# A DLRM tower on one core: gathered rows in buffers of their own, w1 loaded elsewhere, middle shelves by broadcast, and new orders on all engines

## What is computed

```python
e = jnp.stack([tbl_0[ids[:, 0]], ..., tbl_38[ids[:, 38]]], axis=1)   # (2048, 39, 64)
s = jnp.sum(e, axis=-1)                                            # (2048, 39)
z = s[:, _ROW] * s[:, _COL]                                        # all 741 pairs
h = jnp.concatenate([z, dense_ctx], axis=1)                        # (2048, 757)
h = jnp.maximum(h @ W_top1 + b_top1, 0.0)                          # 512
h = jnp.maximum(h @ W_top2 + b_top2, 0.0)                          # 256
y = h @ W_top3
```

## Time and profile before

| | |
|---|---|
| three executions | 318.14, 319.54, 319.74 us |
| profiled execution, span | 314.8 us (its own total isn't given beside it; the median is 4.7 us above the span) |
| TensorE busy | 207.8 us (66%), 1659 matmuls |
| VectorE busy | 144.2 us (46%) |
| ScalarE busy | 81.2 us (26%) |
| GpSimd busy | 114.8 us (36%), of which gathers 112.2 |
| DMA | 43.70 MB, mean 139 GB/s |
| TensorE clock granted, mean | 0.782 of full |

### The profile page before, as it was taken

How to read it: one execution, slowest core, us unless ns; L and a number is a source line. 1 busy time by engine, 2 the same in 40 slices (tenths; PEclk the granted TensorE clock), 3 DMA queues, 4 the chain that set the end, 5 groups by cost and what they waited for, 6 DMA issues and landing times.

```text
span 314.8 us, 4373 instructions
## 1 busy us (share of the span) xinstructions
PE 207.8 (66%) x1659; PEld 126.9 (40%) x1659; DVE 144.2 (46%) x384; ACT 81.2 (26%) x144; POOL 114.8 (36%) x124
## 2 busy tenths in 40 slices
PE   0652102499794321118956988856999999999996
PEld 0310000344131100004613655653566776667784
DVE  2000000157990000002964679561589988968440
ACT  0200010268980000000064224210132424035432
POOL 6777777000077777740473320537310000000000
PEclk9955555589667555555985999977599999999999
DMA  7811131189924132115693676999124029100000
GB/s 290 286 29 30 27 93 25 46 300 413 418 87 129 25 69 89 25 21 186 221 342 121 217 254 218 350 351 244 25 60 150 2 77 275 52 2 2 2 0 0
DMA packets 13557, 43.70 MB, mean 139 GB/s; under 512 B 3216, under 2 KB 4256, under 8 KB 13408
## 3 DMA queue, kind: packets, MB, share of 16 engines
q1 hardware_dynamic: 9392, 39.42, 36.1%
q0 software_dynamic: 3712, 3.81, 5.8%
q10 hardware_dynamic: 432, 0.19, 0.2%
HBM read 43.14 MB, written 0.27 MB: 138 GB/s over the span
## 4 chain that ended last, share of the span: by engine, by line
PE 51%; issue 31%; DVE 7%; ACT 5%; another core or an unknown queue 3%; DMA 2%; ACTq 0%; DVEq 0%
PE g L1119 8%; PE ph L1226 8%; PE ph L1227 7%; PE ph L1230 6%; PE ph L1119 5%; PE s L1205 3%; DVE mid_sums L505 2%; PE g L1165 2%; PE g L1102 2%; PE ph L1246 2%; PE g L1140 2%; DMA stage<-early 2%; PE ph L1250 2%; PE ph L1247 2%
## 5 line engine op out<-in xcount | busy, mean ns | idle before, releaser
L429 POOL DMA_INDIRECT rows<-tab,idc x68 | 65.8, 968 | 77.9 <-DVE w_lo L522 32.8
L438 POOL DMA_INDIRECT rows<-tab,idc x48 | 46.4, 968 | 36.7 <-DVE bsum L587 18.4
L1119 PE MATMUL g<-stage,fc 128*32 128x100 f32 x378 | 27.3, 318 | 41.2 <-issue 40.2
L1119 PE MATMUL ph<-stage,fc 128*32 128x96 f32 (+2 forms) x378 | 20.9, 285 | 39.9 <-issue 30.6
L1226 PE MATMUL ph<-z_hi,w_hi 126*128 126x512 f32 (+1 forms) x96 | 44.8, 467 | 0.0
L536 DVE TENSOR_SCALAR hots<-hots,fc 125x2048 bf16<-125x2048 bf16 x28 | 20.7, 751 | 43.6 <-issue 42.5
L1227 PE MATMUL ph<-z_hi,w_lo 126*128 126x512 f32 (+1 forms) x96 | 39.7, 413 | 0.7 <-issue 0.7
L1230 PE MATMUL ph<-z_lo,w_hi 126*128 126x512 f32 (+1 forms) x96 | 39.3, 409 | 0.0
L1119 PEld LDWEIGHTS g<-stage,fc 128*32 128x32 f32 x378 | 15.8, 139 | 52.6 <-issue 50.9
L1119 PEld LDWEIGHTS ph<-stage,fc 128*32 128x32 f32 x378 | 12.4, 134 | 49.1 <-issue 47.9
L478 DVE CAST mparts<-g 125x100 bf16<-125x100 f32 x3 | 0.8, 262 | 62.4 <-PE g L1119 50.4
(11 more groups left out here) (88 smaller groups left out, 269.0 us busy)
## 6 DMA issues: line engine op xcount, KB each, us to landing
stage<-middle SPq DMA_DIRECT2D x17, 800.0 KB
hots<-shelf_scratch SPq DMA_DIRECT2D x17, 512.0 KB
stage<-early SPq DMA_DIRECT2D x3, 768.0 KB
stage<-middle SPq DMA_DIRECT2D x3, 750.0 KB
stage<-early SPq DMA_DIRECT2D x3, 640.0 KB
rows<-tab,idc POOLq DMA_INDIRECT x116
slot_b<-slot_scratch SPq DMA_DIRECT2D x8, 224.0 KB
stage<-early SPq DMA_DIRECT2D x3, 512.0 KB
```

The costliest lines, as they stand in the source:

```text
L429: pool.indirect_dma_start(rows[:, n % ROW_RING, i, :], None, gathered[i], bass.IndirectOffsetOnAxis(ap=idc[:, n, i:i + 1], axis=0)).then_i ...
L438: pool.indirect_dma_start(rows[:, n % ROW_RING, i, :], None, gathered[i], bass.IndirectOffsetOnAxis(ap=idc[:, n, i:i + 1], axis=0)).then_i ...
L1119: mm = pe.matmul(bank[j * LANE:(j + 1) * LANE, 0:w], band, stage[:, q, (r * 4 + j) * w:(r * 4 + j + 1) * w], start=(x == 0), stop=(x == PA ...
```

## The change

- The gathered rows get buffers of their own: `rows_two` (two buffers of four tiles for the middle tables, chunk by chunk in turn) and `rows_l` (sixteen tiles for the large ones, no reuse). `asum` and `bsum` are doubled. Each tile has its own semaphore.
- Chunk 1's middle gathers wait for all six parts of w1 (before: five). Chunk 2's and 3's middle gathers wait once, for all four sums of the chunk two before; large gathers wait for no sum.
- Raw w1 goes to `factors`, `mid_picked`, `rows_l` and `rows_two[1]` in four transfers, early in SyncE's list; w2 too.
- Middle shelves come by broadcast DMA from a scratch of their own (`mid_scratch`) for all chunks; the five spreads of middle fields on TensorE and their copies on ScalarE go.
- Chunk 2's slots are spread by TensorE and copied by ScalarE, like those of chunks 0 and 1; only chunk 3's come by DMA.
- The lists of all engines are written in another order. Outputs y lie in `rows_l`.

```diff
-        rows = sb("rows", [P, ROW_RING, NL, DIM], F32)
-        asum = sb("asum", [P, TILES, NA], F32)
+        rows_two = [sb(f"rows_m{c}", [P, TILES, NA - SUMMED[c], DIM], F32) if SUMMED[c] < NA else None for c in (0, 1)]
+        rows_m = [rows_two[c % 2][:, :, 0:NA - SUMMED[c], :] if SUMMED[c] < NA else None for c in range(CHUNKS)]
+        rows_l = sb("rows_l", [P, ROW_RING, NB, DIM], F32)
+        asum = sb("asum", [P, 2, TILES, NA], F32)
...
             def load_weights():
-                sp.dma_start(w1_early, w1[:, 0:(KCH - 1) * H1]).then_inc(w1_in, 16)
-                sp.dma_start(w1_raw[KCH - 1], w1[:, (KCH - 1) * H1:]).then_inc(w1_last_in, 16)
+                for k in (0, 1):
+                    sp.dma_start(w1_raw[k], w1[:, k * H1:(k + 1) * H1]).then_inc(w1_in[k], 16)
+                sp.dma_start(w1_mid, w1[:, 2 * H1:5 * H1]).then_inc(w1_in[2], 16)
+                sp.dma_start(w1_raw[5], w1[:, 5 * H1:]).then_inc(w1_in[3], 16)
...
             def load_mid_shelves(c):
-                if SUMMED[c - 1]:
-                    sp.wait_ge(mid_looked_up, (4, 8, 12, 16)[c - 1])
-                sp.wait_ge(shelf_out, 16)
+                if mid_looks(c):
+                    sp.wait_ge(mid_looked_up, mid_looks(c))
+                sp.wait_ge(mid_out, 16)
+                sp.dma_start(mid_hots[:, 0:SUMMED[c], :],
+                             mid_dram[c * NA:c * NA + SUMMED[c], :].rearrange("(o f) n -> o (f n)", o=1)
+                             .partition_broadcast(P)).then_inc(mid_hots_in, 16)
...
-            def fetch_a(c, t):
-                n = c * TILES + t
-                if c == 1 and t == 0:
-                    pool.wait_ge(w1_split, KCH - 1)
-                if c >= 2:
-                    pool.wait_ge(a_summed, n - ROW_RING + 1)
+            def fetch_a(c, a, b):
+                if c == 1:
+                    pool.wait_ge(w1_split, KCH)
+                elif c >= 2:
+                    pool.wait_ge(a_summed, (c - 1) * TILES)
+                for x in range(a, b):
+                    t, i = divmod(x, NA - SUMMED[c])
...
+            def fetch_b(c, a, b):
                 if c >= 2:
-                    pool.wait_ge(b_summed, n - ROW_RING + 1)
+                    pool.wait_ge(w1_split, 5)
...
-SLOT_SPREAD = 2
+SLOT_SPREAD = 3
...
+            load_table(0, 2)
+            load_dense()
+            load_select()
+            load_table(0, 1)
+            load_table(0, 0)
             load_ids()
-            load_table(0, 0)
-            load_table(0, 1)
-            load_table(0, 2)
+            load_mid_ids()
+            load_weights2()
             load_table(0, 3)
+            load_weights()
```

More of the change, by code:

```diff
@@ L257, in hot_loads, with mid_looks @@
             return sum(not spread_group(v // GROUPS, v % GROUPS) for v in range(u % HOTS, u + 1, HOTS))
[L259 to L269, removed]
+        def mid_looks(c):
+            return sum(len(LOOK_PARTS[x]) for x in range(c) if SUMMED[x]) * TILES
         def selects(c, which):
@@ L587, in sum_b @@
-                dve.tensor_reduce(bsum[:, t, 0:NB], rows[:, slot, NA:, :], AX.X, ALU.add).then_inc(b_summed, 1)
+                n = c * TILES + t
+                dve.wait_ge(rows_b_in[n], 16 * NB)
+                dve.tensor_reduce(bsum[:, c % 2, t, 0:NB], rows_l[:, n % ROW_RING, :, :], AX.X, ALU.add).then_inc(b_summed, 1)
             def split_a(c):
                 dve.wait_ge(cleared, 1)
-                dve.wait_ge(a_summed, (c + 1) * TILES)
+                if SUMMED[c] < NA:
+                    dve.wait_ge(a_summed, sum(SUMMED[x] < NA for x in range(c + 1)) * TILES)
@@ L643, in _ @@
+            split_w1(1)
+            hot(0, 2)
+            split_w1(2)
+            split_w1(3)
+            mid_hot(0)
+            split_tables(1)
+            slot_copy(0, 4, G0)
+            sum_a(0, 1)
+            split_w1(4)
+            split_w1(5)
+            pick(0, 1, G1)
+            slot_copy(0, 5, G0)
             hot(0, 3)
-            pick(0, 2, G0)
+            pick(0, 2, G1)
             hot(0, 4)
+            slot_copy(0, 6, G0)
+            hot(0, 5)
+            split_tables(2)
@@ L812, in _ @@
-            mid_pick(3, 0, 0, 5, G1, 13)
-            z_low(2, 3)
-            multiply(2, 5)
-            z_low(2, 4)
-            sum_a(3, 1)
-            z_low(2, 5)
-            dve.wait_ge(mid_picked_ready, 40)
-            mid_pick(3, 1, 0, 5, G0, 14)
+            hot(3, 6)
+            sum_a(3, 1)
+            pick(3, 1, G0)
+            pick(3, 2, G1)
+            z_low(2, 3)
+            z_low(2, 4)
+            multiply(2, 5)
+            sum_a(3, 2)
+            sum_a(3, 3)
+            pick(3, 3, G0)
@@ L820, in _ @@
+            pick(3, 4, G1)
+            z_low(2, 5)
+            pick(3, 5, G0)
+            pick(3, 6, G1)
+            mid_hot(3)
+            sum_b(3, 0)
+            dve.wait_ge(mid_picked_ready, 35)
+            mid_pick(3, 0, 0, 5, G0, 13)
+            multiply(3, 0)
+            multiply(3, 1)
+            dve.wait_ge(mid_picked_ready, 40)
+            mid_pick(3, 1, 0, 5, G1, 14)
+            z_low(3, 0)
+            h1_low(2, 0)
+            h1_low(2, 1)
+            h1_low(2, 2)
             dve.wait_ge(mid_picked_ready, 45)
@@ L1835 @@
     by_field = np.zeros((P, CHUNK), ids.dtype)
+    mid_by_field = np.zeros((CHUNKS * NA, CHUNK), ids.dtype)
     for c in range(CHUNKS):
@@ L1838 @@
         by_field[c * LANE:c * LANE + NE] = part[:, EARLY].T
-        for i in range(SUMMED[c]):
-            by_field[mid_row(c, i)] = part[:, MIDDLE[i]]
+        mid_by_field[c * NA:(c + 1) * NA] = part[:, MIDDLE].T
     by_row = ids[:, MIDDLE + LARGE].reshape(BATCH // P, P, NL).transpose(1, 0, 2)
```

1025 lines of the change are left out of this document (521 added, 504 removed).

## The result

Five executions of the changed kernel took 334.14 us (median; 333.22 to 337.79), five of the kernel before 319.54: ratio 1.049, 95% interval 1.044 to 1.055, so slower by 15 us. I had forecast 322, in a range of 298 to 336. Ratios and their intervals compare the fast executions of each kernel, so where some executions are slow they can differ a little from the ratio of the medians.

A forecast was written before the change was run, and what follows sets the result against it. Bound: TensorE, 181 us at full pace and some 125 us crawling beside gathers. Span 227.1 + 104.6 - 11 - 2.4 = 318.3 us, plus 4.7 outside it 323.0, leaned a microsecond to 322; range 298 to 336.

The forecast's parts named there:

- First block unchanged, 0: First 40 gathers: same start, crawl to 60.4 us, about as many matmuls issued; between -1 and +1 us, taken as 0.
- w1_split at 78.6: Early w1 load lets its rounding end sooner; w1_split reaches six at about 78.6, starting the second block there, not 87.6.
- 28 gathers, then a pause, crawl of 34 us: Second block: 28 gathers to 113.6 us, POOL pauses for chunk 0's sums, resumes near 120.5; TensorE crawls 85.2 to 119.2.
- Third block 24 gathers, 29.0 us, 56 first-layer matmuls in it, worth 10.4 us: Chunk 2's gathers, 120.5 to 150.5 us, crawl 127.1 to 156.1; 56 first-layer matmuls pass inside, which took 10.4 us before.
- Fourth block at 191.5, 29.0 us, the main loss: Chunk 3's 24 gathers, 191.5 to 221.5 us, crawl 29.0 us, where before small groups cost 15.2 us.
- Credit for matmuls inside, -11 in the fourth block, -10 in all: Matmuls passing inside crawls save later time: 56 in the fourth, 11 us; some 50 more than before in all, -10 us.
- rival 1: Fourth block lets nothing useful through, as matmuls wait for ScalarE and VectorE; without the 11 us credit 333 us; chance 0.17.
- Clock, -2.4: A 4.8 us stretch at granted clock 0.50 right after a crawl that goes away there: 2.4 us back.
- Orders, 0 with -7 to +7: New orders of hots and multiplies on the engines: taken as 0, kept at -7 to +7 us.
- Rival 2: No pause after 28 gathers: 52 run to 143.6 us, crawl to 149.2; +10, 332 us; chance 0.07.
- Rival 3: Crawl goes by gathers, not by block, 0.92 us each, so 24 cost 22 rather than 29; 300 us; chance 0.29.
- Rival 4: Crawl isn't the gathers': it stays with 98 us in two stretches, reordering worth -7 to +7; 319.5 us; chance 0.07.

The follow-up runs named there:

- first trace: Profiled execution of the changed kernel from the first measurement, no edit: span 336.0 us, 337.79 us in all.
- chip 4: Both kernels run again, no edit, on the chip where gathers go with slow stretches: before 317.9 us, changed 334.06 us, ratio 1.050; spans 317.3 and 331.0.
- the first pair: Profiled executions of the kernel before and the changed one from the first measurement: spans 314.8 and 336.0 us; medians 319.54 and 334.14 us.
- chips 13 and 1: Changed kernel with chunk 3's gathers tile by tile (edit idle), 201.5 us, ratio 1.016; changed kernel unedited, 201.5 us against 199.6, ratio 1.020.

## Why the prediction was right and wrong

The measured 334.14 us lies in the range of 298 to 336, near its upper end, and the sign held. The sign alone is no success: I had given 0.45 to slower and 0.42 to faster, and forecast 2.5 us of loss where there are 14.6. What held is the mechanism as far as the slow stretches go: four blocks, their places in the order and what they cost. What failed is what I let pass inside them. Set against the forecast's own milestones, in us:

| part | forecast | first trace | chip 4 |
|---|---|---|---|
| start to the third crawl | 127.1 | 130.9 (+3.8) | 130.0 (+2.9) |
| third crawl | 29.0 | 29.4 (+0.4) | 27.4 (-1.6) |
| from there to the fourth crawl | 42.0 | 50.7 (+8.7) | 50.6 (+8.6) |
| fourth crawl | 29.0 | 29.9 (+0.9) | 27.9 (-1.1) |
| rest | 91.2 | 95.1 (+3.9) | 95.1 (+3.9) |
| span | 318.3 | 336.0 (+17.7) | 331.0 (+12.7) |

On chip 4 two terms, +8.6 and +3.9, are all but 0.2 us of the miss, and both stand where I had credited matmuls inside a block.

- *First block unchanged, 0.* Its end moved from 60.4 to 61.5 (60.8 to 62.0 on chip 4): 1.1 and 1.2 us later, just over my 1.
- *w1_split at 78.6.* The second block began at 80.22, and at 78.29 on chip 4. Right.
- *28 gathers, then a pause, crawl of 34 us.* 28, a pause, 34.2 us (32.6 on chip 4). Right. But POOL resumed at 129.15 (128.09 on chip 4), not 120.5. **This step failed.** I had TensorE recovered at 119.2 and took POOL to resume a microsecond later, though two quarters of the middle table and a look still stood ahead of the pick before the fourth sum. They could have passed inside the block only if its crawl let some 73 matmuls through. It let 39 through, 34 on chip 4. That 73 might pass came from a misreading of my own rows. I had "64 in 28 us", but those 28 us began with the block's first gather, and TensorE had started 44 of the 64 at full pace ahead of the crawl. From the onset on, the same trace has 57 in 34 us (47 on chip 4), nearly all of them sums that wait for nobody:

```profile
92.72 1.22 PE L1119 MATMUL g<-stage,fc 128*32 128x100 f32 x44
...
94.00:128.00 34.00, 10.31 (x57) 3.66 (x57) 0.86 (x2) 0.00 (x0) 25.77 (x28) 0.57 0.27 74
```

  Why the new block lets fewer still through is open. In the first trace TensorE's wait of 18.5 us for ScalarE would explain it, but on chip 4 there is no such wait and 34 pass. The step cost 3.8 and 2.9 us.
- *Third block 24 gathers, 29.0 us, 56 first-layer matmuls in it, worth 10.4 us.* 29.4 us and 17 matmuls (27.4 and 18 on chip 4), none of them of the first layer. **This is the largest miss.** The first-layer matmuls, which before go on at 145.62 and were to be 18.5 us ahead of that, start at 164.75, 19 us behind it (158.00 on chip 4). So they stand behind the block and not in it: 50.7 us for 42.0.
- *Fourth block at 191.5, 29.0 us, the main loss.* It began at 206.84 (202.61 on chip 4) and its crawl took 29.9 us (27.9). Its cost over the groups of before was to be 29.0 - 15.2 = 13.8. On chip 4 it was +13.9, by the account above. Right in size.
- *Credit for matmuls inside, -11 in the fourth block, -10 in all.* The sign that I had named for rival 1, under 50 matmuls in the fourth crawl, came: 42, and 36 on chip 4. Behind the first block 98 pass instead of 126 (88 instead of 117), where I had some 50 more. Not the whole credit is gone, though. Without it and with nothing else changed the rest would be some 102 us, an estimate (91.2 + 11), and it is 95.1. Rival 1's 333 us is close to the measured time, but by another route: the largest part of the miss comes from the third block.
- *Clock, -2.4.* The stretch behind the fourth block is at 0.98 of full clock, as expected; but the one behind the second is at 0.57 and the first 7.7 us behind the third at 0.50, so the lower level was moved rather than saved.
- *Orders, 0 with -7 to +7.* +2 to +4 us where nothing crawls (with all else that the change does); on chip 4, what isn't slow stretches didn't grow. Inside.

Rival 2 did not happen (a pause came after 28). Rival 3, crawl by gathers at 0.92 us each wherever they stand, is refuted on chip 4 and in the first pair: blocks of 28 and 24 cost 1.14 to 1.25 each (32.6 and 34.2, 27.4 to 29.9), and groups of three cost nothing in either trace of before. That is why 24 in one block cost more than in groups. Rival 4 said that the crawl is not the gathers'. Where the earlier trace rows had five coincidences, the four blocks of the changed kernel add four more, three of them in new places, and no slow stretch stands apart from a block. But no kernel without gathers ran where there is a crawl, so that they cause it is argued and not shown; and on chips 13 and 1 all 116 gathers in a row leave TensorE alone. That agrees with the Trainium skill ("SBUF — State Buffer", section "SBUF: two separate sides"): gathers have no need to slow matmuls. On chip 4 the matmuls are slow beside them; by what path no run shows.

Open: why chip 4 behaves so, and whether other chips do; whether the crawl there goes when the gathers go; whether spacing them out saves its time (the last 24 say that it might, 14 us); what in the new orders costs 2 us.

## What to carry to other kernels

When a profile shows an engine waiting for nothing, time the kernel on a second chip before moving work around: here 119 of 318 us were there on one chip of five, and the change would have been judged by them. To price work inside a slow stretch, count from the moment when the engine slows and not from the event that you hold responsible: 44 of my 64 matmuls had gone before. Give little credit for what passes inside, even where the rows of before show more: here 98 matmuls for a forecast of 177. And cut the kernel at a few milestones of its own, such as the four y stages: they show where the time was lost, with no judgement about where a slow stretch begins.

## What the hardware showed unexpectedly

- The same program takes 318 us on one chip and 197 to 201 on four, with the same gathers at 1.25 us each. It isn't the clock: in the first slow stretch of the chip 4 traces the granted clock is 1.00 of full.
- Beside gathers in a row, in the slow traces, an engine goes on late after another's work: 17 us for y, in both traces of the changed kernel (228.21 and 225.35), and the shelf spreads that TensorE started at 96.14 and 98.32 are copied from 120.31. Whether the signal is late or ScalarE itself, the traces can't tell apart.
- TensorE's first gap put down to "issue" begins 1.7 to 4.3 us after the first gather of the last three blocks (81.99, 130.86 and 211.10 us), not 6.6. In the changed kernel's traces the crawl ends 3 to 6 us after the last gather of the first, second and fourth block, but within 1.5 us of the third's. In the fourth block it eased for 3.7 us at 228.2, in mid block, which I can't explain.
- Beside small memsets by GpSimd, eight in 0.28 us, a VectorE instruction can last until the whole string is over: a one-hot that starts at 39.37 beside memsets that end at 46.04 takes 7.21 us, two casts at 60.13 and 113.39 take 3.95 and 6.36. Others keep their time: a cast at 38.77, beside the same memsets, takes 0.68.

```profile
39.37 7.21 DVE L588 TENSOR_SCALAR hots<-hots,fc 125x2048 bf16<-125x2048 bf16 x1
```
